# Reordering the attention stage of a perceiver layer, and moving the scan's second half into the feed-forward block

## The reference

```python
x = x + xattn(layernorm(x), ctx)          # stage 1
x = x + ssm(layernorm(x))                 # gate in stage 1, scan and layer norm behind it
x = x + ffn(layernorm(x))                 # stage 3

# xattn: Sim = hc@w1 + ctx@w2 + (hc*w3)@ctx.T + b ; A = softmax(Sim) ; hq = A@ctx
#        Batt = softmax(max(Sim)) over tokens ; hb = sum(Batt*hc)
#        out = concat[hc, hq, hc*hq, hc*hb] @ W_qv + b_qv
# ssm:   xg = z*sigmoid(z@Wg.T + bg) ; s = s@A + xg*Bp ; y = s.Cp + Dp*xg ; out = layernorm(y + xg)*gamma + beta
# ffn:   h = bitlinear(x, w_fc) + gate*(x@v.T@fast_b.T@u.T) ; out = bitlinear(relu(h)**2, w_proj)
# bitlinear: weights rounded to -1, 0, 1 times their row's mean magnitude
```

## Time and profile before

| | us |
|---|---|
| three runs | 538.26, 539.46, 541.32 |
| median | 539.46 |
| profiled execution, its own time | 538.2 |
| its span, first to last instruction | 536.0 |
| busy: PE, PEld, DVE | 479.5, 402.3, 419.3 |
| busy: ACT, POOL | 359.2, 343.7 |

### The profile page before, as it was taken

How to read it: one execution, slowest core, us unless ns; L and a number is a source line. 1 busy time by engine, 2 the same in 40 slices (tenths; PEclk the granted TensorE clock), 3 DMA queues, 4 the chain that set the end, 5 groups by cost and what they waited for, 6 DMA issues and landing times. The chain is left out here.

```text
span 536.0 us, 13439 instructions
## 1 busy us (share of the span) xinstructions
PE 479.5 (89%) x4310; PEld 402.3 (75%) x4310; DVE 419.3 (78%) x1159; ACT 359.2 (67%) x854; POOL 343.7 (64%) x444
## 2 busy tenths in 40 slices
PE   3397899999999999999999978947799999999996
PEld 2275687878887877687787867836588888888885
DVE  1488988888888999999998875375677987988654
ACT  2565578676776767677676767645578768768753
POOL 2377767676775757756756654502578878888653
PEclk9789899999999999999999999988899999999999
DMA  6634355756484564555555668385203033021102
GB/s 213 191 117 153 118 164 161 218 161 215 141 235 135 179 167 133 198 145 137 197 140 144 194 200 175 67 205 180 90 1 80 1 80 79 27 55 39 41 1 78
DMA packets 77972, 70.38 MB, mean 131 GB/s; under 512 B 40000, under 2 KB 60752, under 8 KB 77392
## 3 DMA queue, kind: packets, MB, share of 16 engines
q1 hardware_dynamic: 77904, 69.54, 45.5%
HBM read 56.87 MB, written 12.65 MB: 130 GB/s over the span
## 5 line engine op out<-in xcount | busy, mean ns | idle before, releaser
L1668 POOL TENSOR_TENSOR sq_lo<-scan_x,sq_hi 128x512 fp32r<-128x512 f32 x63 | 82.7, 1312 | 33.4 <-ACT sq_hi L1640 33.4
L718 PE MATMUL turn_ps<-ident,ctxn 128*128 128x128 f32 x512 | 71.2, 284 | 4.3 <-DMA ctxn<-in_ctx 4.3
L718 PEld LDWEIGHTS turn_ps<-ident,ctxn 128*128 128x128 f32 x512 | 59.0, 145 | 18.2 <-issue 13.6
L946 ACT COPY ctxT<-turn_ps 128x512 f32<-128x512 f32 x128 | 68.1, 582 | 5.4 <-PE turn_ps L718 5.4
L1632 ACT ACTIVATE relu<-fc_ps,fc_square 128x512 f32<-128x512 f32 x64 | 43.8, 684 | 31.3 <-PE fc_ps L1566 31.2
L1134 POOL TENSOR_TENSOR hc_lo<-hc_probT,hc_hi 128x256 fp32r<-128x256 f32 x32 | 23.3, 729 | 64.0 <-ACT hc_hi L953 64.0
L1710 DVE SCALAR_TENSOR_TENSOR scan_x<-fc_ps,relu 128x512 f32<-128x512 f32 x64 | 43.8, 684 | 26.2 <-ACT relu L1632 25.7
L1562 PE MATMUL fc_ps<-xn_hi,fc_T 128*128 128x512 f32 x128 | 52.1, 407 | 2.1 <-DVE scan_x L1710 2.1
L1120 POOL TENSOR_TENSOR rstd<-ve,neg_half 128x1 f32<-128x1 f32 x64 | 35.2, 549 | 25.6 <-DVE ve L1353 15.6
L1562 PE MATMUL fc_ps<-xn_lo,fc_T 128*128 128x512 f32 x128 | 51.1, 400 | 0.0
L1126 POOL TENSOR_TENSOR proj_in<-proj_in,below 128x512 f32<-128x512 f32 x31 | 49.2, 1587 | 0.0
(11 more groups left out here) (227 smaller groups left out, 1398.8 us busy)
## 6 DMA issues: line engine op xcount, KB each, us to landing
ctxn<-in_ctx SPq DMA_DIRECT2D x32, 1024.0 KB, 5.5
resid<-in_x SPq DMA_DIRECT2D x32, 128.0 KB, 5.2
ctx_end<-in_ctx SPq DMA_DIRECT2D x32, 128.0 KB
gated_tokens<-gated SPq DMA_DIRECT2D x32, 128.0 KB, 6.2
scan_x<-gated_tokens SPq DMA_DIRECT2D x60, 64.0 KB, 4.8
out<-resid SPq DMA_DIRECT2D x7, 512.0 KB, 3.3
scan_quarters<-scan_x SPq DMA_DIRECT2D x3, 1024.0 KB, 4.6
y_in<-scan_quarters SPq DMA_DIRECT2D x16, 128.0 KB, 3.0
```

The source lines that it names most:

```text
L718: mm = pe.transpose(turn_ps[b % 2][:, (c * JT + t) * P:(c * JT + t + 1) * P], ctxn[p][:, b, t, c * P:(c + 1) * P], ident[:, :])
L946: act.copy(ctxT[:, b, :, 0:J - 1], turn_ps[b % 2][:, :].rearrange("p (k j) -> p k j", k=KD)).then_inc(ctxT_copied, 1)
L1668: pool.tensor_tensor(sq_lo[:, m, :], sq[m % SQ], sq_hi[:, m, :].bitcast(F32), ALU.subtract).then_inc(sq_lo_done, 1)
```

## The change

- **Stage 1, order.** PE turns hc at the end of the step before, apart from the probabilities; attend is followed directly by score; the product with hb comes before the gate, that with hq and hcq after it. ACT, DVE and POOL are reordered to match. `gated` of a group is made one step later.
- **Gate in fp32r**: six fp32r matmuls in place of one fp32 product per K half; new are zT_hi, zT_lo (DVE) and wgT_hi, wgT_lo.
- **Three context buffers**; the third lies in the first quarter of `toeplitz`, which is zeroed in eighths, six in steps 4 to 9 and the two lent ones in step 31.
- **Exponentials stay in PSUM**: the exponential is written over `score_ps`, and `prob` is made from there; the mask for `pick` lies in PSUM too.
- **Spread work**: ternary rows one instruction a step in steps 17 to 32; states two a step only in steps 3, 4, 5; load order at the start, with the wait for W_qv alone.
- **The passage**: the stage's block ends after scan block 7 and seven weight turns; proj_T's turns, blocks 8 to 15 and chunk 0's layer norms come in the next block. Chunk 0 is taken through them in halves, and chunk 1's centring and adding follow in chunk 0's tiles. The loads of groups 30 and 31 go behind both store halves and the block's end.
- **Stage 3**: chunks 1 and 2 are turned after tiles 6 and 5, their low-rank products before the next chunk's tile 0; `sq_hi` and `sq_lo` have 6 buffers, `xn_hi` and `xn_lo` 2 chunks.

```diff
@@ load order and waits at the start
                 load_x(0)
+                load_ctx(0)
...
-                load_ctx(0, 0)
...
+                sp.dma_start(wqv_raw, W_qv.rearrange("(k p) n -> p k n", p=P)).then_inc(wide_loaded, 16)
...
+                    if g == 1:
+                        act.wait_ge(wide_loaded, 16)
+                        act.copy(wqv_hi, wqv_raw).then_inc(wqv_hi_ready, 1)
...
-                    if isinstance(g, int) and g == 0:
-                        act.wait_ge(late_loaded, 16 * LATE)
-                        act.copy(wqv_hi, wqv_raw).then_inc(wqv_hi_ready, 1)
@@ PE, one step
+                    if has_a:
+                        at_least(pe, ctx_loaded[g % DEEP], 16 * (g // DEEP + 1))
+                        turn_context(g, 0)
+                        turn_context(g, 1)
                     if has_b:
+                        turn_prob(g)
...
+                        pool_hc(g)
+                    if has_b and g > 1:
+                        project_hc(g)
+                    if has_a:
+                        turn_context(g, 2)
+                        turn_context(g, 3)
...
+                        attend(g)
                     if has_a:
+                        score(g)
...
+                        turn_z(g - 2)
...
+                        project((hb_hi, hb_lo), 3, hb_lo_ready, g)
+                    if g + 1 < GROUPS:
+                        turn_hc(g + 1)
                     if has_c:
+                        sum_gate(g - 2)
                     if has_b:
                         at_least(pe, hq_hi_ready, g)
+                        project((hq_hi, hq_lo), 1, hq_lo_ready, g)
                         at_least(pe, hcq_hi_ready, g)
+                        project((hcq_hi, hcq_lo), 2, hcq_lo_ready, g, last=True).then_inc(projected, 1)
@@ sum_gate
+                    for i, (part, w) in enumerate(((zT_hi, wgT_hi), (zT_hi, wgT_lo), (zT_lo, wgT_hi))):
+                        for c in range(KD):
+                            mm = pe.matmul(gate_ps[:, 0:D], part[:, c, :], w[:, c, :], start=(i == 0 and c == 0),
+                                           stop=(i == 2 and c == KD - 1))
@@ the exponential (ACT) and the probabilities (DVE)
-                        act.activation(prob[p][:, :], score_ps[:, 0:J], ACT.Exp, bias=neg_max[:, 0:1],
+                        act.activation(score_ps[:, 0:J], score_ps[:, 0:J], ACT.Exp, bias=neg_max[:, 0:1],
-                        dve.tensor_scalar(prob[p][:, :], prob[p][:, :], row_rec[:, 0:1], None, ALU.mult
+                        dve.tensor_scalar(prob[p][:, :], score_ps[:, 0:J], row_rec[:, 0:1], None, ALU.mult
@@ DVE: new in every step, and ternary rows
+                        dve.tensor_tensor(zT_lo[:, :, :], gate_ps[:, 256:256 + D].rearrange("p (k t) -> p k t", k=KD),
+                                          zT_hi[:, :, :].bitcast(F32), ALU.subtract).then_inc(zT_lo_ready, 1)
-                    if TERNARY <= g < TERNARY + MT:
-                        m = g - TERNARY
-                        ternary(dve, fc_in[:, m, :], m, fc_temp, 1, m)
+                    if TERNARY <= g < TERNARY + 2 * MT:
+                        m, second = divmod(g - TERNARY, 2)
+                        (ternary_above if second else ternary_below)(dve, fc_in[:, m, :], m, fc_temp, 1, m)
@@ SP at the end of stage 1
-                sp.wait_ge(gated_stored[0], 16 * (GROUPS // 2))
-                scan_load(sp, GROUPS - 2, 1)
                 sp.wait_ge(scan_copied, BLOCKS)
                 store_half(sp, 0)
+                step(GROUPS + 1, 0, ())
                 store_half(sp, 1)
                 sp.wait_ge(first_stored[0], 16 * NB)
                 y_load(sp, 0)
@@ SP in the next block
+                for g in (GROUPS - 2, GROUPS - 1):
+                    sp.wait_ge(gated_stored[g % 2], 16 * (GROUPS // 2))
+                    scan_load(sp, g, 1)
+                sp.wait_ge(first_stored[1], 16 * NB)
+                y_load(sp, 1)
@@ PE in the next block
+                for turn in range(7, 11):
+                    turn_proj(turn)
+                for n in range(2 * BLOCKS, PIECES * BLOCKS):
+                    last_scan(n)
+                turn_first()
                 low_rank(0)
@@ DVE in the next block
+                first_y(dve)
+                first_x(dve)
+                y_sums(dve, 1, range(CH))
...
+                second_centre(dve)
...
+                        if c == 0 and m < 2:
+                            second_add(dve, m)
@@ first_x: per half add, statistics; then both halves of xn (first_y is built alike)
+            for h in range(2):
+                dve.wait_ge(centred, h + 1)
+                dve.wait_ge(rstd_y_done, h + 1)
+                for r in half(h):
+                    ins = dve.scalar_tensor_tensor(out=res(0, r), in0=y_in[:, r, :], scalar=rstd_y[:, r:r + 1],
+                                                   in1=res(0, r), op0=ALU.mult, op1=ALU.add)
+                ins.then_inc(x2_done, 1)
...
+            for h in range(2):
+                dve.wait_ge(rstd_x_done, h + 1)
+                for r in half(h):
+                    ins = dve.tensor_scalar(xn[:, r, :], res(0, r), mv_x[:, r, 0:1], rstd_x[:, r:r + 1],
+                                            ALU.subtract, ALU.mult)
+                ins.then_inc(xn_done, 1)
```

More of the change, by code:

```diff
@@ new lines, in attend @@
+                def attend(g):
+                    at_least(pe, prob_copied, g)
+                    at_least(pe, hq_ready, g - 1)
+                    at_least(pe, dot_done, min_groups(g + 1))
+                    for t in range(JT):
+                        for b in range(NB):
+                            mm = pe.matmul(att_ps[b * L:(b + 1) * L, 0:D], hc_probT[g % 2][:, 1, t, b * L:(b + 1) * L],
+                                           ctxn[(g - 1) % DEEP][:, b, t, :], start=(t == 0), stop=(t == JT - 1))
+                    mm.then_inc(attended, 1)
@@ new lines, in score @@
+                def score(g):
+                    at_least(pe, ctxT_copied, g * 4 + 4)
+                    at_least(pe, end_placed, g + 1)
+                    at_least(pe, hcwT_ready, g + 1)
+                    at_least(pe, neg_max_ready, g)
+                    at_least(pe, prob_ready, g)
+                    for c in range(KD):
+                        for b in range(NB):
+                            mm = pe.matmul(score_ps[b * L:(b + 1) * L, 0:J], hcwT[:, c, b * L:(b + 1) * L],
+                                           ctxT[:, b, c, :], start=(c == 0), stop=(c == KD - 1))
+                    mm.then_inc(scored, 1)
@@ new lines, in weigh_hc @@
+                def weigh_hc(g):
+                    if g == 0:
+                        act.wait_ge(consts_loaded, 16 * CONSTS)
+                    at_least(act, scored, g)
+                    act.wait_ge(hc_copied, g + 1)
+                    for c in range(KD):
+                        ins = act.activation(hcwT[:, c, :], hc_probT[g % 2][:, 0, c, :], ACT.Identity,
+                                             bias=w23[:, 0, c:c + 1], scale=w23[:, 1, c:c + 1])
+                    ins.then_inc(hcwT_ready, 1)
@@ L1146, in add_bqv, with zero, place_high, step @@
                     pool.tensor_tensor(r, r, bqv_all[:, :], ALU.add).then_inc(bqv_added, 1)
-                def step(base, k, state_steps):
-                    g, p, has_a, has_b, has_c = stages(base, k)
-                    inside = not isinstance(g, int)
-                    o = 1 - p
+                def zero(part):
+                    rows = CQ // ZERO_PARTS
+                    pool.memset(toeplitz[:, part * rows:(part + 1) * rows, :], 0.0).then_inc(zeroed, 1)
+                def place_high(q, h):
+                    pool.wait_ge(zeroed, ZERO_PARTS)
+                    pool.wait_ge(windows_loaded[h], 16 * NB)
+                    pool.tensor_copy(*place(q, h)).then_inc(high_placed, 1)
+                    pool.wait_ge(high_placed, 2 * h + q - 1)
+                def step(g):
+                    p, o = g % 2, 1 - g % 2
+                    has_a, has_b, has_c = g < GROUPS, 1 <= g <= GROUPS, g >= 2
+                    if has_b:
+                        low_part(hc_lo[:, :, :], hc_probT[o][:, 0, :, :], hc_hi[:, :, :], hc_hi_ready, hc_lo_ready, g)
+                    if has_c:
+                        at_least(pool, z_ready, g - 2)
+                        inverse_deviation(rstd2[:, :], ve2[:, :], ve2_done, rstd2_done, g - 1)
                     if has_a:
-                        if not inside and g == 0:
+                        if g == 0:
                             pool.wait_ge(endsT_ready, 1)
```

1062 lines of the change are left out of this document (553 added, 509 removed).

## The result

The changed kernel takes 525.25 us (median of 4 runs, 523.81 to 527.94) where the kernel before takes 539.2 (median of 4 beside it); the ratio is 0.9742 with a 95% interval of 0.9692 to 0.9791. It is faster by 14 us. The forecast was 504.5 with a range of 493 to 521: the direction was right, the size was not, and the range missed it.

A forecast was written before the change was run, and what follows sets the result against it. PE was taken to bound ordinary stage 1 and the feed-forward stage, with losses at the start, ternary steps and passage. -8 - 23 - 5.5 + 1.5 = -35 gave 503.2, or 504.5 us on the median's scale, range 493 to 521.

The forecast's parts named there:

- Part 4: Stage 3: PE stays the bound; later turns and chunk 1's added DVE work cost +1.5 us, bounds 0 and +4.
- only four matmuls to hide in: Stage 3, chunks 0 and 1: the low-rank result has little PE work to cover it; included in the +1.5 us.
- Part 2: Stage 1's 30 steps between exponentials: 271.5 us against 294.4, so -23 us, bounds -32 and -10.6.
- The ordinary step: Stage 1: a step without extras falls from 9.13 to 8.85 us, with PE staying the bound.
- Narrow blocks side by side: Stage 1, PE: attend next to score pays the weight-load wait once, -0.2 us a step, between 0 and -0.41.
- the term of 6 us for steps with extras: Stage 1: doubled states, magnitudes, low-rank work and impulse response add 6 us together over the 30 steps.
- A long `hc`: Stage 1, DVE: hc was to take 0.41 us in all steps; a longer one would show the forecast wrong.
- The three buffers: Stage 1 context loads: three buffers were costed at nothing, as PE waits for no context load in ordinary steps.
- Part 1: The start, up to group 1's exponential: less waiting for W_qv saves 8 us, bounds -4.5 and -10.
- Part 3: The passage from stage 1 to stage 3: hidden products start 5.5 us earlier, bounds 0 and -8.
- DVE as the bound: Rival, stage 1: DVE needs 9.7 us in 16 steps, adding 13.6 us, for 518 us; chance 0.2.
- The slower rival: Stage 1: waits in the chain from scores to turned probabilities lengthen steps; steps of 10.3 us give 548; chance 0.03.

The follow-up runs named there:

- experiment 1: Against the changed kernel, both halves of ACT's norm_y(2) moved behind split_hi(1), at tile 7 of chunk 0 in stage 3; 520.63 us.
- experiment 5: Against the changed kernel, norm_y(2) behind split_hi(1) and both times_gamma(2) at tile 7 of chunk 0, ahead of square_lo(0,7); 516.96 us.
- the regular chunk 1: Also the best kernel: changed kernel with norm_y, times_gamma, impulse and low_in moved, plus chunk 1 using later chunks' places for turn, low-rank product and layer norms; 510.13 us.
- experiments 1 to 5: Against the changed kernel, places of norm_y(2), times_gamma(2) or add_y(2) in stage 3 moved, singly or combined; 520.63, 525.63, 520.21, 526.3 and 516.96 us.
- experiments 6, 7 and 8: Each against the changed kernel: impulse-response work moved later, 524.07 us; low_in moved from step 20 to 31, 521.62 us; exponential back in SBUF, 542.31 us.
- experiment 8: Against the changed kernel, the exponential writes prob in SBUF and DVE scales it there, instead of reading PSUM; 542.31 us.

## Why the prediction was wrong, step by step

- **Part 4, stage 3: the step that failed.** Forecast +1.5, bounds 0 and +4; measured +14.9. I weighed the late turn by PE's own time between turn and use, and DVE's 3.3 us by its sum. What I didn't do is walk the queues of ACT, POOL and DVE through the first two chunks and ask what stands behind each new wait. Three placements made most of it, each shown by a kernel that moves it: `norm_y(2)` ahead of the split, 3.6 us (experiment 1); `times_gamma(2)` behind a `square_lo` that is itself waiting, 3.3 (experiment 5); the late turn and low-rank product of chunk 2 with the layer norms that go with them, 2.9 (the regular chunk 1; which of these it was, no run tells apart). About 2 us more are this execution's own, 1.6 of them the fallen clock. Some 3 us remain: the best kernel still takes 162.8 us from the first hidden product to the end, 159.85 before. Of these, 2.3 lie in its chunk 1 (7 tiles in 19.19 us, where before 8 take 19.0 and a tile is 2.1), and the largest wait there is the 1.56 us for the low-rank result of chunk 1; the prediction had named that term ("only four matmuls to hide in") and sized it too small. Moving that product as well was not tried.
- **Part 2, the steps.** The ordinary step came as forecast: 8.89 (8.85), 9.13 before. `hc` at 0.40 and `zT_lo` at 0.415 were right. `prob` from PSUM took 0.487, not 0.41, and is short in every step. Narrow blocks side by side: 0.22, forecast 0.2. Wrong was the term of 6 us for steps with extras: the 30 steps take 12.6 us more than 30 × 8.89 (10.1 to 12.7 in the executions of experiments 1 to 5, which have the same stage 1). The step to exponential 21 has 3.5 of it (undone: 0; 1.6 are the clock), those to 29 and 30 1.9 and 1.4, those with a doubled state 1.8, the one to exponential 2 2.6. In three of these places DVE worked on SBUF operands beside a long POOL instruction, the very contention that I had credited as gone for `hc`; I hadn't followed POOL's order into the steps that differ. A long `hc` was one of the signs named for a wrong forecast, and it came in four steps (1.40 and 2.23 us).
- **The three buffers.** The prediction put them at nothing, and the kernel as changed has no such wait. But without the third the kernel is some 32 us slower (557.6 against 525.25), so the three carry the gain of Part 2 just as the exponential in PSUM does (17 us).
- **Part 1, the start.** -6.2 in this execution; in the others group 1's exponential came between 24.0 and 27.7, so the forecast of 24 was its fast end.
- **Part 3, the passage.** From the last product of stage 1 (317.62) to the hidden products 33.4 us; forecast 33, before 38.2. Only 0.9 us went the other way ahead of it, as PE waits 2.4 us for ACT's z of the last group.
- **The rivals.** DVE as the bound (518) was nearest in time, but for the wrong reason: in the ternary steps PE is busy 61.91 of 62.00. The slower rival didn't come.

The Trainium skill's rule on the shared SBUF interfaces (GPSIMD Engine Reference, Key points) fits experiments 6, 7 and 8: 2.23 against 0.40 us, 1.48 against 0.29, 2.58 against 0.35. Its rule on PSUM operands (VectorE: DVE Perf Modes, "Why PSUM operands drop a tier") is right for the undisturbed instruction (0.35 us from SBUF in experiment 8, 0.487 from PSUM), but the kernel is 17 us slower with the SBUF form, because POOL works beside it.

## What to carry to other kernels

When work is moved into an in-order queue, don't price it by its duration: for each instruction that waits, list what stands behind it and who waits for that, chunk by chunk where the chunks differ; here 9.8 us hung on three placements. A rare long step is worth a look by itself, for beside a long POOL instruction a short DVE one on SBUF can take over five times its time. And what "costs nothing" may still be what the rest of the change stands on: undo it once before calling it free. When a marker instruction measures a stretch, check that the same work lies between two marks in both kernels; and before a difference of one profiled stretch is put down to an edit, look at the granted clock there.

## What the hardware showed

- A DVE instruction on fp32 operands in SBUF, started with or behind one of POOL's, ended 0.14 to 0.15 us behind it: `hc` of 0.40 us took 2.23 and 1.40, the last operation of `low_in` 1.48 instead of 0.29, `prob` 2.58 instead of 0.35. In the last case it outlasted two POOL instructions that followed each other, a product of 1.55 us and a memset of 0.97.
- The change between 32- and 128-column tiles on TensorE cost 0.10 us entering and 0.12 leaving.
- The granted clock fell to its lower level behind a wait of 1.7 to 1.8 us in some executions of the same code and not in others, at two places (the step to exponential 21 and chunk 1), for 1.6 us each time. That made an edit without effect look like a gain of 2 us.
